# The order of the last down products, and two of the last norms, in a transformer block on one core

## The reference

```
x = layernorm(x + attention(x))
g = x @ Wg.T ; u = x @ Wu.T          # Wg, Wu: 2048 x 512, (integer - 128) * scale of the row
h = silu(g) * u                      # 512 tokens x 2048
out = layernorm(x + h @ Wd.T)        # Wd: 512 x 2048
```

## Time and profile before

| | us |
|---|---|
| median of three runs | 780.61 |
| the profiled execution itself | 784.28 |
| its span, first to last instruction | 782.1 |
| TensorE busy (mean granted clock 0.98) | 744.8 |
| VectorE busy | 395.1 |
| ScalarE busy | 387.4 |
| GpSimd busy | 128.2 |

### The profile page before, as it was taken

One profiled execution on the slowest core, in us unless ns is written; L12 is line 12 of the kernel. 1 busy time (PEld: TensorE's weight loads), 2 busy tenths in 40 slices (PEclk: granted clock), 3 DMA queues, 4 the chain that ended last, 5 costly groups with the idle time before them and its releaser, 6 DMA issues.

```text
span 782.1 us, 11953 instructions
## 1 busy us (share of the span) xinstructions
PE 744.8 (95%) x4480; PEld 571.0 (73%) x4480; DVE 395.1 (51%) x1006; ACT 387.4 (50%) x914; POOL 128.2 (16%) x148
## 2 busy tenths in 40 slices
PE   7998899999999999999899999899999999999993
PEld 6776576776767677776578887688887888788882
DVE  4755666567566666567542222353326432463236
ACT  3754766666766666676555655422224222322220
POOL 0000110315131050301834123200000000000001
PEclk9999899999999999999899999999999999999997
DMA  9201413335521364302568954511210010000201
GB/s 316 89 0 28 135 59 77 81 83 122 151 79 55 88 183 136 73 12 73 124 148 184 224 176 139 178 63 40 68 55 0 13 58 36 0 1 27 81 1 55
DMA packets 59719, 68.67 MB, mean 88 GB/s; under 512 B 33552, under 2 KB 35600, under 8 KB 59536
## 3 DMA queue, kind: packets, MB, share of 16 engines
q1 hardware_dynamic: 53456, 49.05, 21.0%
q0 software_dynamic: 6208, 18.88, 10.2%
HBM read 59.53 MB, written 14.68 MB: 95 GB/s over the span
## 4 chain that ended last, share of the span: by engine, by line
PE 90%; DVE 4%; ACT 3%; issue 1%; DMA 1%; POOLq 0%; SPq 0%; POOL 0%; DVEq 0%; ACTq 0%
PE bank L1365 15%; PE bank L1366 15%; PE bank L1158 12%; PE bank L1234 9%; PE bank L1371 7%; PE bank L1372 7%; PE bank L1173 6%; PE bank L1217 5%; PE bank L1255 5%; PE bank L1192 5%; ACT probs L710 1%; DVE probs L917 1%; PE bank L1266 1%; PE bank L1130 1%; PE bank L1120 1%
## 5 line engine op out<-in xcount | busy, mean ns | idle before, releaser
L710 ACT ACTIVATE probs<-probs,neg_max 128x128 f32<-128x128 f32 (+3 forms) x256 | 140.4, 552 | 12.7 <-DVE neg_max L917 12.7
L1033 DVE SCALAR_TENSOR_TENSOR hid<-bank,u_scale,silu 128x512 f32<-128x512 f32 x64 | 48.1, 751 | 176.2 <-PE bank L1366 174.1
L917 DVE CUSTOM_DVE_ANT_0 probs<-bank,causal 128x128 f32<-128x128 f32 (+3 forms) x256 | 111.6, 484 | 29.1 <-PE bank L1217 27.8
L1365 PE MATMUL bank<-xT_hi,gateT 128*128 128x512 f32 x256 | 101.9, 398 | 5.7 <-DVE xT_lo L1042 3.8
L823 ACT ACTIVATE hid_hi<-hid 128x512 fp32r<-128x512 f32 x64 | 40.5, 632 | 122.5 <-DVE hid L1033 122.5
L1366 PE MATMUL bank<-xT_lo,gateT 128*128 128x512 f32 x256 | 101.1, 395 | 0.0
L1371 PE MATMUL bank<-downT,hid_hi 128*128 128x512 f32 x256 | 99.9, 390 | 0.9 <-DVE hid_lo L1036 0.8
L1365 PE MATMUL bank<-xT_hi,upT 128*128 128x512 f32 x256 | 100.3, 392 | 0.0
L1366 PE MATMUL bank<-xT_lo,upT 128*128 128x512 f32 x256 | 100.1, 391 | 0.0
L1372 PE MATMUL bank<-downT,hid_lo 128*128 128x512 f32 x256 | 99.7, 389 | 0.0
L1234 PEld LDWEIGHTS bank<-ident,probs 128*128 128x128 f32 x640 | 75.0, 144 | 30.5 <-issue 15.8
(11 more groups left out here) (94 smaller groups left out, 1137.5 us busy)
## 6 DMA issues: line engine op xcount, KB each, us to landing
scan_buf<-in_L_ffn_gate_w_dram SPq DMA_DIRECT2D x4, 1024.0 KB, 5.1
scan_buf<-in_L_ffn_up_w_dram SPq DMA_DIRECT2D x4, 1024.0 KB, 5.2
scan_buf<-in_L_ffn_down_w_dram SPq DMA_DIRECT2D x4, 1024.0 KB, 5.2
y_scratch<-z_tok SPq DMA_DIRECT2D x16, 256.0 KB, 5.0
x_tok<-y_scratch SPq DMA_DIRECT2D x4, 1024.0 KB, 6.1
w_int<-in_L_ffn_gate_w_dram POOLq DMA_DIRECT2D x16, 256.0 KB, 3.1
w_int<-in_L_ffn_up_w_dram POOLq DMA_DIRECT2D x16, 256.0 KB, 2.9
w_int<-in_L_ffn_down_w_dram POOLq DMA_DIRECT2D x16, 256.0 KB, 3.8
```

The source lines that it names most:

```text
L710: nc.scalar.activation(probs[qb][:, j, :], probs[qb][:, j, :], ACT.Exp, bias=neg_max[:, qb, j:j + 1], scale=-1.0, accum_out=row_sum[:, qb, ...
L917: nc.vector.tensor_tensor_reduce(out=probs[qb][:, j, :], in0=score[j][:, first:first + w], in1=causal[:, S - w:S], scale=-SCALE, scalar=-F ...
L1033: nc.vector.scalar_tensor_tensor(out=hid[:, i % 2, :], in0=bank[:, :], scalar=u_scale[:, i:i + 1], in1=silu[:, i % 2, :], op0=ALU.mult, op ...
L1365: nc.tensor.matmul(acc[n][:, :], w[:, c, cols], form(xT_hi[:, c, :]), start=c == 0, stop=False)
```

## The change

Three edits, in the last batch only.

- A table `HELD` says for each token tile from which row tile on its down products wait for the end: 15, 11, 10 and 6. `down` of the last batch does in the stream, for each token tile, what lies below that, and without a count on `down_full`. At the end TensorE first does token tile 3's row tiles 6 to 10, waits for the last hidden tile, then finishes tiles 0, 1, 2 and 3. The number of products is the same.
- For this, row tiles 6 to 11 of the last batch get places of their own, `hid_hi_more` and `hid_lo_more`, laid over memory that staged weights used in batch 0. `hid_place` chooses the place.
- VectorE no longer norms token tiles 0 and 1 (`QH` = 2). GpSimd does so behind each one's root. VectorE does the norms of tiles 2 and 3 behind the last variance, after a wait for GpSimd's two. `drain_down` waits for the count of its tile in the new numbering of `down_full`.

```diff
--- before.py
+++ after.py
@@ -210,6 +210,10 @@
     WEIGHTS = [p for p in PIECES if p[0] != "y"]
     INTS = 2
     HIDS = NT
+
+
+    HELD = [NI - 1, NI - 5, NI - 6, NI - 10]
+    MORE_FIRST, KEPT_FIRST = HELD[-1], NI - HIDS
     LEVEL_FRONT, LEVEL_INVERSE, LEVEL_PROBS = 40, 16, 24
     SHIFTS = 2
     CHUNKS = NI // TPR
@@ -297,6 +301,10 @@
         third.close()
         yT_next = sb("yT_next", [P, ND, S], F32, ffn)
         d_scaled = sb("d_scaled", [P, NT, D], F32, ffn)
+        kept = ExitStack()
+        hid_hi_more = sb("hid_hi_more", [P, KEPT_FIRST - MORE_FIRST, S], F32R, kept)
+        hid_lo_more = sb("hid_lo_more", [P, KEPT_FIRST - MORE_FIRST, S], F32R, kept)
+        kept.close()
         stage_0 = sb("stage_0", [P, 3, ND, TPR * P], BF16, ffn)
         stage_1 = sb("stage_1", [P, 3, ND, TPR * P], BF16, ffn)
         stage = [stage_0, stage_1, stage_2, stage_0]
@@ -415,6 +423,12 @@
                 return downT[:, TPR * n:TPR * (n + 1), piece[2] * P:(piece[2] + 1) * P]
             return yT_next[:, n, :].rearrange("p (t q) -> p t q", t=NT)
 
+        def hid_place(b, i):
+
+            if isinstance(b, int) and b == LAST and MORE_FIRST <= i < KEPT_FIRST:
+                return hid_hi_more[:, i - MORE_FIRST, :], hid_lo_more[:, i - MORE_FIRST, :]
+            return hid_hi[:, i % HIDS, :], hid_lo[:, i % HIDS, :]
+
         def full_by(n, weights):
 
             return n + 1 if weights is wide_weights else sum(piece[0] == "y" for piece in PIECES[:n + 1])
@@ -684,6 +698,10 @@
                 pool.wait_ge(var2_done, B + t)
                 nc.gpsimd.tensor_tensor(ln_rstd[:, t:t + 1], ln_var[:, t:t + 1], half_power[:, t:t + 1],
                                         ALU.pow).then_inc(rstd2_done, 1)
+                if t < QH:
+                    pool.wait_ge(rstd2_done, LAST + t + 1)
+                    nc.gpsimd.tensor_scalar(z_tok[:, t, :], z_tok[:, t, :], ln_mv[:, t, 0:1], ln_rstd[:, t:t + 1],
+                                            ALU.subtract, ALU.mult).then_inc(out_done, 1)
 
         @block.scalar
         def _(act):
@@ -820,7 +838,7 @@
             def hidden_hi(b, i):
                 act.wait_ge(hid_done, b * NI + i + 1)
 
-                nc.scalar.activation(hid_hi[:, i % HIDS, :], hid[:, i % 2, :], ACT.Copy).then_inc(hid_hi_done, 1)
+                nc.scalar.activation(hid_place(b, i)[0], hid[:, i % 2, :], ACT.Copy).then_inc(hid_hi_done, 1)
 
             def y_hi(b):
 
@@ -1033,8 +1051,8 @@
                 nc.vector.scalar_tensor_tensor(out=hid[:, i % 2, :], in0=bank[:, :], scalar=u_scale[:, i:i + 1],
                                                in1=silu[:, i % 2, :], op0=ALU.mult, op1=ALU.mult).then_inc(hid_done, 1)
                 dve.wait_ge(hid_hi_done, b * NI + i + 1)
-                nc.vector.tensor_tensor(hid_lo[:, i % HIDS, :], hid[:, i % 2, :], hid_hi[:, i % HIDS, :].bitcast(F32),
-                                        ALU.subtract).then_inc(hid_ready, 1)
+                hi, lo = hid_place(b, i)
+                nc.vector.tensor_tensor(lo, hid[:, i % 2, :], hi.bitcast(F32), ALU.subtract).then_inc(hid_ready, 1)
 
             def y_lo(b):
                 for c in range(ND):
@@ -1044,7 +1062,7 @@
 
             def drain_down(b, t):
 
-                dve.wait_ge(down_full, (b + 1) * NI - (NT - 1 - t if isinstance(b, int) and b == LAST else 0))
+                dve.wait_ge(down_full, LAST * NI + t + 1 if isinstance(b, int) and b == LAST else (b + 1) * NI)
                 nc.vector.tensor_tensor(d_scaled[:, t, :], down_acc[t][:, :], d_scale[:, :], ALU.mult).then_inc(d_done, 1)
 
             def add_residual(b, t):
@@ -1094,9 +1112,10 @@
                 add_residual(LAST, t)
                 dve.wait_ge(mv2_done, LAST * NT + t + 1)
                 nc.vector.tensor_scalar(ln_var[:, t:t + 1], ln_mv[:, t, 1:2], EPS, None, ALU.add).then_inc(var2_done, 1)
-                if t > 0:
-                    apply_norm(LAST + t - 1, t - 1, rstd2_done, out_done)
-            apply_norm(LAST + NT - 1, NT - 1, rstd2_done, out_done)
+
+            dve.wait_ge(out_done, LAST * NT + QH)
+            for t in range(QH, NT):
+                apply_norm(LAST + t, t, rstd2_done, out_done)
 
         @block.tensor
         def _(pe):
@@ -1368,8 +1387,9 @@
 
                 def down_block(b, i, t):
                     tok = slice(t * P, (t + 1) * P)
-                    nc.tensor.matmul(down_acc[t][:, :], form(hid_hi[:, i % HIDS, tok]), w_down[:, i, :], start=i == 0, stop=False)
-                    return nc.tensor.matmul(down_acc[t][:, :], form(hid_lo[:, i % HIDS, tok]), w_down[:, i, :], start=False,
+                    hi, lo = hid_place(b, i)
+                    nc.tensor.matmul(down_acc[t][:, :], form(hi[:, tok]), w_down[:, i, :], start=i == 0, stop=False)
+                    return nc.tensor.matmul(down_acc[t][:, :], form(lo[:, tok]), w_down[:, i, :], start=False,
                                             stop=i == NI - 1)
 
                 def down(b, i):
@@ -1382,6 +1402,11 @@
                             for t in range(NT):
                                 wait_drained(pe, "o", B - 1, t)
                             pe.wait_ge(normed, GROUPS)
+                    if isinstance(b, int) and b == LAST:
+                        for t in range(NT):
+                            if i < HELD[t]:
+                                down_block(b, i, t)
+                        return
                     for t in range(NT):
                         last = down_block(b, i, t)
                     last.then_inc(down_full, 1)
@@ -1427,7 +1452,7 @@
                                 transpose_y(b + 1, c, (gate_acc, up_acc)[c % 2][n % 2]).then_inc(yT_full, 1)
                             continue
                         gate_up(b, i, n % 2, lambda c: pe.wait_ge(yT_done, (b - 1) * ND + c + 1))
-                        if i >= 1 and (ahead or i - 1 < NI - NT):
+                        if i >= 1:
                             down(b, i - 1)
                     if ahead:
                         down(b, NI - 1)
@@ -1436,13 +1461,13 @@
                     ffn_batch(b, True)
                 ffn_batch(B - 1, False)
 
-                for t in range(2):
-                    for i in range(NI - NT, NI - 1):
-                        pe.wait_ge(hid_ready, LAST * NI + i + 1)
-                        down_block(LAST, i, t)
+
+                pe.wait_ge(hid_ready, LAST * NI + NI - 1)
+                for i in range(HELD[-1], HELD[1]):
+                    down_block(LAST, i, NT - 1)
                 pe.wait_ge(hid_ready, LAST * NI + NI)
                 for t in range(NT):
-                    for i in range(NI - 1 if t < 2 else NI - NT, NI):
+                    for i in range(HELD[t] if t < NT - 1 else HELD[1], NI):
                         last = down_block(LAST, i, t)
                     last.then_inc(down_full, 1)
 
```

## The result

The changed kernel takes 777.17 us (median of 20 runs) against 781.27 for the kernel before in the same comparison: ratio 0.9948, 95% interval 0.9932 to 0.9964, 4.1 us faster. The forecast was 3.95 us and 776.7. The profiled execution took 774.96 us with a span of 773.0, 9.1 us less than the span before. That is more than the change is worth, and the trace shows how it splits: 4.1 us in the tail, and 5.0 us ahead of the first instruction that the change touches, where the two executions differ in their stretches of low granted clock.

The account below looks back on a forecast made before the run. TensorE bounds the kernel (busy 744.8 of 782.1 us), but VectorE's four output tiles bound its end. 3.18 us (earlier start) plus 0.87 (two norms) is 4.05, minus 0.1 (adds) 3.95: 780.61 - 3.95 = 776.7 us, range 775.6 to 777.7.

Parts of the forecast that it names:

- Part 1: Order of the down products: net 7 pairs fewer ahead of the last gate/up product, first drain 3.18 us earlier.
- Part 2: VectorE's four last tiles: drains 2.54 us apart, two norms off its chain save 0.87 us, VectorE stays the bound.
- Part 3: POOL's two norms of 2.06 us each in the tail: delayed roots stay off the path, cover 1.1 us.
- The unknown: POOL's norm beside VectorE's add, both in SBUF: 0 to 0.9 us for two adds, taken as 0.1 us.
- the later one waited: Ground for pricing SBUF overlap: POOL, starting 0.18 us after the add, waits; both adds together cost 0.1 us.
- rival A: VectorE's two adds beside POOL norms pay 0.33 to 0.44 us each whatever the order; 777.3 us, chance 0.25.
- C: POOL's norm gets in first and holds adds of tiles 1 and 2 throughout; 780.8 us, one add 778.7; chance 0.08.
- D: Some wait keeps the first drain at 764.9, only the norms' 0.87 us remain; 779.7 us, chance 0.07.
- B: TensorE or POOL turns late in the tail: gain 3.2 to 3.6 us, 777.2 us, chance 0.08.
- The sum: Whole tail: 4.05 us gained minus 0.1 for the adds, 3.95 us, giving 776.7 us; forecast chance 0.52.
- the offset of one execution from the median: Profiled run lies 3.67 us above the timed runs' median, taken as equal for both kernels.

Follow-up runs that it names:

- experiment 1: Changed kernel with POOL's norms taken out, all four on VectorE one tile behind as before, leaving only the new order of down products; ratio 0.9946.
- experiment 2: Kernel before with its matmul order kept, only the norms of token tiles 0 and 1 moved to POOL and the others behind the last variance; ratio 0.9987.
- held_seven: Changed kernel with one more pair of matmuls of token tile 2 held back, seven instead of six; ratio 0.9937.
- pool_three: Changed kernel with the norm of token tile 2 on POOL too, VectorE doing only the last; ratio 0.9961.
- norm_first_2: Changed kernel with an unused 256-column VectorE product between drain and add of token tiles 1 and 2; 778.78 us in one execution.

## Why the prediction was right

**Part 1** (the first drain 3.18 us earlier): 3.17 in the trace, and experiment 1 has it alone. The pairs were counted right, no cover was broken: the sixth pair still hides the last hidden tile's chain, and the stream with one pair between products has no gap.
**Part 2** (tiles 2.54 us apart, 0.87 from two norms): 2.53 and 0.89, experiment 2 alone has 0.89. The margin of 0.09 us between tile 2's matmuls and its drain was real: held_seven took 0.45 us from it and met a wait of 0.23 us.
**Part 3** (POOL's cover 1.1 us): of that, 0.52 us was left (766.30 to 766.82). The 1.1 was drawn with a root 1 of 0.55 and a first norm of 2.06. They took 0.95 us more together; some 0.4 of this came back because POOL's instructions followed each other about 0.1 us closer than drawn. A third norm (pool_three) overran the cover.
**The unknown**: priced 0.1 us of 0 to 0.9, it cost nothing on VectorE. For tiles 1 and 2 it went as drawn: POOL was the later one and waited, 0.49 us of it in its first norm. But the ground, "the later one waited", was read from two rows and doesn't hold in general. By it tile 3's add would have paid: it was drawn to meet only the end of POOL's second norm, lay wholly in it instead, began 1.30 us later than it, and took 0.69. In norm_first_2 the later one didn't wait either. That these cost nothing was luck. Had I priced the add by the `hid_lo` row in full (rival A), the forecast would have been 3.2. The rule of the Trainium skill ("SBUF — State Buffer", SBUF: two separate sides), that the first holds the port for its whole instruction, would in norm_first_2 have kept the add back by 2 us; the trace has an add of 0.69 us there. Where the add came first the traces agree with it: POOL waited the add out.
**Rivals.** A, C and D are excluded: no add took over 0.69 us, and the drain moved. B came only where a pair or a norm was added. **The sum** of 3.95 us against 4.06 in the tail and 4.1 in the timed runs: the difference is the 0.1 for the adds. The timed 4.1 alone, with an interval of 2.8 to 5.3, couldn't tell this.
**What missed** is the profiled execution itself: drawn with a span near 778.1, it had 773.0, 5.1 us less. The prediction took the offset of one execution from the median as equal for both kernels. It has no word on why runs scatter by 7 us: I took three runs' spread as a bound on what can be told, and didn't look at the clock's stretches.

## What to carry to other kernels

When a serial chain on a vector engine ends a kernel behind a stream of matmuls, give each output tile its last product as late as the chain will take it, and no later: the order of equal work was worth 3.2 us here, and the limit is where the last tile's matmuls and the chain meet. Offload to a second engine only what its own queue has room for: two norms fitted here and three did not. Measure such a gain from an event just ahead of the change, and after adding even a tile of 16 bytes look whether the matmuls far from it still take as long.

## What was not expected of the hardware

- Where the weight tiles lie changes the matmuls' pace: 32 bytes up or 128 down cost on average 7 and 5 ns on some 390 per gate/up matmul and, by the ratios 1.0078 and 1.0048 beside 0.9948, 10 and 8 us of the kernel. That it is the weight tiles' own address, and not that of another tile that moved with them, is likely but not shown.
- Executions of one kernel differ by up to 7 us. In the fourteen traces, one for each kernel, the lower clock comes ahead of the tail in stretches of 3.4 or 6.8 us near 85, 380, 405 and 498 us, not all of them in every trace, 10.2 to 23.8 us in all. What TensorE did just before doesn't tell the two kernels apart: from 78.0 to 84.8 us it was busy 3.66 us in the kernel before, whose clock then fell to half, and 3.47 us in the changed kernel, whose clock stayed full.
- POOL's norm and root, begun 0.1 us behind a VectorE add with two SBUF operands, took 0.49 and 0.46 us more: POOL waits the add out. An add begun 1.30 us inside a POOL norm cost neither engine anything. No VectorE add of any tail paid; `hid_lo`, 0.16 to 0.18 us inside a norm, paid 0.44 in every trace.
